# Two-layer graph network on one core: when GpSimd's inner products and VectorE's turned one-hot run in the second sweep

## The chip, the cores and the metric

One core of a Trainium2 chip. The metric is the device time of one execution in microseconds; less is better. Every engine of the core (TensorE, VectorE, ScalarE, GpSimd, SyncE) runs its own list of instructions in order, and the lists are tied together by semaphores alone. In the profile they are called PE (with PEld for its weight loads), DVE, ACT, POOL and SP.

## The reference

20,000 directed edges join 1,250 nodes with 512 features each. Layer 0 is an attention sum over edges; layer 1 is a message layer whose features are 128 scalars and 128 vectors of three components. Each is added to its input and normalized. The second sweep computes, for every edge, the part of layer 1 below:

```python
ip1 = jnp.einsum('eum,eum->eu', p1[edge_dst], p1[edge_src]) / 3.0
s0 = jnp.concatenate([pd0, pd0, ip1], axis=-1)
...
w = ssp(edge_attr @ W_f1) @ W_f2 * (ssp(s0 @ W_s1) @ W_s2)
w1, w2, w3, w4 = jnp.split(w, 4, axis=-1)
x0e, x1e = split_irreps(x[edge_src])
out0 = w1 * x0e * sh0[:, None] + w4 * (jnp.einsum('eum,em->eu', x1e, sh1) / jnp.sqrt(3.0))
out1 = w2[:, :, None] * x0e[:, :, None] * sh1[:, None, :] + w3[:, :, None] * x1e * sh0[:, None, None]
out = jax.ops.segment_sum(edge_feat, edge_dst, num_segments=old_x.shape[0])
```

`ssp` is softplus minus log 2. The names edge_dst and edge_src are the two ends of an edge: sums go to the one, features are gathered from the other. Everything is float32.

## The kernel before

The kernel first sorts the edges into groups: 88 groups of 256 slots, each group with edges of one block of 128 receiving nodes only. A slot is an edge or is empty. After the sort come the first sweep (layer 0), a stage over nodes that writes a table of 896 numbers for each node to DRAM (`tab_d`), the second sweep (layer 1), and a last stage over nodes.

The second sweep does the 88 groups one after another; a group is two tiles of 128 edges (index k). A step of a group g is a small function on one engine, and the helper `pipelined` writes the steps out in a fixed order. For its iteration i it goes through the engine's list of pairs (lag, step) and issues step(i - lag). So the order in the list is the order in the engine's queue, and lag says how many iterations a step stands behind. The loop is unrolled by U = 8.

The steps that matter here, with their lines:

- SyncE, `load`: the edges' data (`ed`), their receiving nodes turned to run along the free dimension (`ilb`), and features (`hcat`), eight groups ahead.
- GpSimd, `gather` (line 1028): two indirect DMAs fetch the table rows of the 256 source nodes into a ring of R = 4 groups (`xj`, in the tensor `ring`). `dots` (lines 1037, 1040, 1042): one product and two additions make the inner product of the vector part with the edge's three components, into `dot`, two groups deep.
- TensorE: `sources` (line 1095) spreads the receiving nodes' vectors over the edges, using the turned one-hot; `inner` (line 1054) transposes and adds VectorE's products; `hidden` (1081, 1083); `factors` (1108); `sums` (1066, 1068, 1070) adds up messages by receiving node with the one-hots as weights.
- ScalarE: `factor_out` (1151) copies a factor from PSUM, `inner_out`, `log_part` (softplus in parts), and `scaled_rows` (1121), six scaled copies of the one-hots.
- VectorE, in the order of its queue: `one_hot` (lines 1205 and 1206, two instructions for each of two tiles, SBUF to SBUF), `weights` (1174), `messages` (1181, 1184, 1189, the last of which needs `dot`), `softplus` (1169), `accumulate` (1196, adds TensorE's sums to `acc`), `turned_one_hot` (1215, `ohT` from `ilb`, SBUF to SBUF), `products` (1164, PSUM times the gathered rows, for `inner`).

The lags: in VectorE's iteration i stand one_hot, weights and messages of group i-3, softplus of i-2, accumulate of i-4, turned_one_hot of i, products of i-1. In GpSimd's iteration i stand gather of i and dots of i-2. What ties GpSimd to the others is this:

```python
if not first(g, R):
    gp.wait_ge(msg_ready, g - (R - 1))     # in gather: its ring slot is free
...
gp.wait_ge(xj_in[c], n * 32)               # in dots: the rows have landed
after(gp, msg_ready, g - 1)                # dot's buffer is free
```

`after(engine, semaphore, count)` waits until the semaphore has reached count, and does nothing for a count known to be zero or less. `oh_ready` goes up by one when a group's four one-hot instructions are done, `msg_ready` when its last message instruction is. `accumulate` waits for `sum_ready`, which TensorE raises at the end of `sums`; `products` waits for the gathered rows (`xj_in`) and for `pi_ready` of `sources`.

Of the kernel before, what the change touches and what calls it, by code (L numbers as in the profile page):

```python
# [30 lines left out]
U = 8  # L31
# [10 lines left out]
def build(nc, x, src, dst, edge_rows, W, b, a, W_pre0, b_pre0, W_pre1, W_nd0, b_nd0, W_nd1, W_g1, b_g1,  # L42
          W_g2, b_g2, W_f1, W_f2, W_s1, W_s2, W_o0, b_o0, W_o1, out):
    ctx = ExitStack()
    with ctx:
        def sb(name, shape, dt=F32, scope=ctx):
            return scope.enter_context(nc.sbuf_tensor(name, shape, dt))

        def sem(name):
            return ctx.enter_context(nc.semaphore(name))  # L50

        def after(eng, s_, count):

            if not (isinstance(count, int) and count <= 0):
                eng.wait_ge(s_, count)
# [43 lines left out]
        ring = sb("ring", [P, max(R * 2 * TW, U * 2 * XT)])  # L99
# [464 lines left out]
        def pipelined(eng, *stages, count=NG, turn=U, ring=R):  # L564


            last = max(lag for lag, _ in stages)
            peel = turn * max(-(-last // turn), 1)
            for i in range(peel):
                for lag, step in stages:  # L570
                    if i >= lag:
                        step(i - lag, (i - lag) % turn, (i - lag) // ring + 1)
            with eng.Fori(0, (count - peel) // turn) as j:  # L573
                for i in range(turn):
                    for lag, step in stages:
                        g0 = peel + i - lag
                        step(j * turn + g0, g0 % turn, j * (turn // ring) + (g0 // ring + 1))
            for i in range(count, count + last):
                for lag, step in stages:
                    if i - lag < count:  # L580
                        step(i - lag, (i - lag) % turn, (i - lag) // ring + 1)
# [5 lines left out]
        def first(g, m):  # L587
            return isinstance(g, int) and g < m
# [385 lines left out]
        oh_ready = sem("oh_ready")  # L974
# [26 lines left out]
        with nc.Block() as block:  # L1001
# [15 lines left out]
            @block.gpsimd  # L1017
            def _(gp):
                def gather(g, c, n):
                    r = c % R  # L1020

                    gp.wait_ge(ed2[c], n * 64)
                    gp.sem_inc(issue2, 1)
                    if not first(g, R):
                        gp.wait_ge(msg_ready, g - (R - 1))
                        gp.sem_inc(issue2, 1)
                    for k in range(2):
                        gp.indirect_dma_start(xj[:, r, k, :], None, tab_d[:, :],  # L1028
                                              bass.IndirectOffsetOnAxis(ap=ed[:, c, k, JD:JD + 1].bitcast(I32), axis=0))\
                          .then_inc(xj_in[c], 16)  # L1030

                def dots(g, c, n):

                    r, u = c % R, c % 2
                    gp.wait_ge(xj_in[c], n * 32)
                    after(gp, msg_ready, g - 1)
                    gp.tensor_tensor(dot[:, u, :, :, :], xj[:, r, :, P:D].rearrange("p k (m n) -> p k m n", m=3),  # L1037
                                     ed[:, c, :, IL + 2:IL + 5].unsqueeze(3).to_broadcast([P, 2, 3, P]), ALU.mult).then_inc(dot_mul, 1)
                    gp.wait_ge(dot_mul, g + 1)
                    gp.tensor_tensor(dot[:, u, :, 0, :], dot[:, u, :, 0, :], dot[:, u, :, 1, :], ALU.add).then_inc(dot_add, 1)  # L1040
                    gp.wait_ge(dot_add, g + 1)
                    gp.tensor_tensor(dot[:, u, :, 0, :], dot[:, u, :, 0, :], dot[:, u, :, 2, :], ALU.add).then_inc(dot_ready, 1)
                pipelined(gp, (0, gather), (2, dots), ring=U)

            @block.tensor
            def _(pe):
# [110 lines left out]
            @block.vector  # L1157
            def _(v):
                def products(g, c, n):
                    r = c % R  # L1160
                    v.wait_ge(xj_in[c], n * 32)
                    v.wait_ge(pi_ready, g + 1)
                    after(v, ip_ready, g)
                    v.tensor_tensor(prod[:, :, :], psB, xj[:, r, :, D:TW], ALU.mult).then_inc(prod_ready, 1)  # L1164

                def softplus(g, c, n):

                    v.wait_ge(ln_done, g + 1)
                    v.scalar_tensor_tensor(hcat[0:2 * HID, c, :], psH, 0.0, lx[:, :], ALU.max, ALU.add).then_inc(sp_done, 1)  # L1169

                def weights(g, c, n):

                    v.wait_ge(s_copied, g + 1)
                    v.tensor_tensor(psF, S_sb[:, :, :], psF, ALU.mult).then_inc(w_done, 1)  # L1174

                def messages(g, c, n):
                    r, u = c % R, c % 2

                    v.wait_ge(w_done, g + 1)
                    after(v, sum_ready, g - 1)  # L1180
                    v.tensor_tensor(mm_sb[:, u, :, 0:D + P].rearrange("p k (s n) -> p k s n", n=P)[:, :, 0:5:4, :],
                                    psF[:, :, 0:2 * P].rearrange("p k (s n) -> p k s n", n=P),
                                    xj[:, r, :, 0:P].unsqueeze(2).to_broadcast([P, 2, 2, P]), ALU.mult)
                    v.tensor_tensor(mm_sb[:, u, :, P:D].rearrange("p k (m n) -> p k m n", m=3),  # L1184
                                    psF[:, :, 2 * P:3 * P].unsqueeze(2).to_broadcast([P, 2, 3, P]),
                                    xj[:, r, :, P:D].rearrange("p k (m n) -> p k m n", m=3), ALU.mult)

                    v.wait_ge(dot_ready, g + 1)
                    v.tensor_tensor(mm_sb[:, u, :, D + P:D + 2 * P], psF[:, :, 3 * P:D], dot[:, u, :, 0, :], ALU.mult).then_inc(msg_ready, 1)  # L1189

                def accumulate(g, c, n):
                    blk_r = v.value_load(gblk[0:1, bass.ds(g, 1)], min_val=0, max_val=NB - 1)
                    v.wait_ge(sum_ready, g + 1)
                    after(v, acc2_done, g)
                    dst_ = acc[:, bass.ds(blk_r, 1), 0:D].rearrange("p b n -> p (b n)")
                    v.tensor_tensor(dst_, dst_, psA, ALU.add).then_inc(acc2_done, 1)  # L1196

                def one_hot(g, c, n):

                    u = c % 2  # L1200
                    v.wait_ge(ed2[c], n * 64)
                    after(v, oh_sh_ready, g - 1)
                    after(v, sum_ready, g - 1)
                    for k in range(2):
                        v.tensor_scalar(oh[:, u, k, :], iota[:, :], ed[:, c, k, IL:IL + 1], None, ALU.is_equal)  # L1205
                        ins = v.tensor_scalar(ohs[:, u, k, 0, :], iota[:, :], ed[:, c, k, IL:IL + 1], ed[:, c, k, IL + 1:IL + 2],  # L1206
                                              ALU.is_equal, ALU.mult)
                    ins.then_inc(oh_ready, 1)

                def turned_one_hot(g, c, n):  # L1210

                    u = c % 2
                    v.wait_ge(ed2[c], n * 64)
                    after(v, hid_ready, g - 1)
                    v.tensor_scalar(ohT[:, u, :], ilb[:, c, :], pcol[:, 0:1], None, ALU.is_equal).then_inc(ohT_ready, 1)
                pipelined(v, (3, one_hot), (3, weights), (3, messages), (2, softplus), (4, accumulate), (0, turned_one_hot),
                          (1, products), ring=U)


# [139 lines left out]
```

## Time and profile before

| | before |
|---|---|
| median of 3 runs | 1291.41 us (1288.12 to 1293.72) |
| profiled execution | 1291.39 us |
| its span in the profile | 1289.7 us |
| TensorE busy, whole span | 999.7 us, 78% |
| VectorE busy | 939.1 us, 73% |
| ScalarE busy | 546.3 us, 42% |
| GpSimd busy | 794.0 us, 62% |

The page of the profile gives busy times over the whole span. The second sweep runs from about 555 us to about 1245 us of it; a table by stretches cuts such a part out. A round is the time from one group's step to the next group's same step. A line in a timeline has the start in us, the duration in us, engine, line, operation, output and inputs, the count of merged instructions, and in brackets the idle time of the engine before it with what ended it.

### The profile page before, as it was taken

Reading aid. Unit: us, or ns where it says so; the run is one execution under the profiler, and the core shown is the slowest. Engines: PE = TensorE matmul, PEld = TensorE weight load, DVE = VectorE, ACT = ScalarE, POOL = GpSimd, SP = SyncE. Lnnn points to the kernel's source line nnn. Section 1 sums busy time; section 2 is a strip of 40 time slices with the busy share of each in tenths; the row PEclk is TensorE's granted clock in tenths of the full one; section 3 lists DMA queues with packets and bytes.
Section 4 is the critical chain, followed back from the end, with each engine's and each line's share of the span. In section 5 each row is a group of like instructions: output and inputs, shape, how many; then the busy total and the mean of one; then the engine's idle time right before and its main releaser. Section 6 shows DMA issues by size and latency. Waiting matters only on the chain. (4 is left out here: it accounts for less than half of the span.)

```text
span 1289.7 us, 23680 instructions
## 1 busy us (share of the span) xinstructions
PE 999.7 (78%) x5530; PEld 643.5 (50%) x5531; DVE 939.1 (73%) x2190; ACT 546.3 (42%) x1559; POOL 794.0 (62%) x809
## 2 busy tenths in 40 slices
PE   2227445499999967748999889999999999998874
PEld 1213222255555546625656555565565655655554
DVE  7250101378777758538999999989999899999967
ACT  2213210123233326525555555555555555555541
POOL 3777777577777711256666666666666666666622
PEclk9757678699999989859999999999999999999997
DMA  9201101588777831154544444544444444444302
GB/s 346 57 15 32 32 23 57 146 242 241 238 241 237 242 66 57 66 191 149 155 145 139 139 144 148 158 141 143 151 151 143 142 148 149 153 141 139 114 1 82
DMA packets 109167, 177.46 MB, mean 138 GB/s; under 512 B 40191, under 2 KB 79343, under 8 KB 109009
## 3 DMA queue, kind: packets, MB, share of 16 engines
q0 software_dynamic: 33184, 130.15, 31.3%
q1 hardware_dynamic: 72752, 45.60, 12.3%
q10 hardware_dynamic: 3200, 1.38, 0.5%
q8 instruction: 11, 0.18, 0.1%
q14 instruction: 20, 0.16, 0.0%
HBM read 157.31 MB, written 19.74 MB: 137 GB/s over the span
## 5 line engine op out<-in xcount | busy, mean ns | idle before, releaser
L1028 POOL DMA_INDIRECT ring<-tab_d,ed x176 | 181.4, 1030 | 232.8 <-DVE mm_sb L1189 168.7
L698 PE MATMUL ps<-ring,aw 128*128 128x512 f32 x352 | 195.7, 644 | 18.6 <-DVE aw L649 16.9
L618 POOL DMA_INDIRECT ring<-xt_d,ed x176 | 168.0, 955 | 61.4 <-issue 43.9
L1121 ACT ACTIVATE ohs<-oh,ed 128x128 f32<-128x128 f32 x528 | 171.7, 389 | 77.2 <-DVE ohs L1206 77.1
L375 POOL DMA_INDIRECT slots_d<-stage,stage_pos x157 | 153.5, 978 | 66.3 <-issue 48.7
L1066 PE MATMUL ps<-mm_sb,ohs 128*128 128x512 f32 x352 | 189.4, 620 | 1.4 <-DVE acc L1196 1.4
L1068 PEld LDWEIGHTS ps<-mm_sb,ohs 128*128 128x128 f32 x1056 | 145.6, 191 | 84.3 <-issue 84.3
L1151 ACT ACTIVATE S_sb<-ps 128x512 f32<-128x512 f32 x176 | 95.5, 595 | 132.0 <-PE ps L1108 132.0
L1068 PE MATMUL ps<-mm_sb,ohs 128*128 128x128 f32 x1056 | 146.2, 275 | 0.0
L1037 POOL TENSOR_TENSOR dot<-ring,ed 128x768 f32<-128x768 f32 x88 | 130.3, 1480 | 10.2 <-DVE mm_sb L1189 7.3
L1108 PE MATMUL ps<-w,hcat 32*128 32x512 f32 x704 | 102.0, 648 | 27.1 <-DVE hcat L1169 27.1
L1054 PEld LDWEIGHTS ps<-ident,prod 128*128 128x128 f32 x528 | 57.7, 143 | 119.8 <-DVE prod L1164 106.5
L1054 PE MATMUL ps<-ident,prod 128*128 128x128 f32 x528 | 78.7, 286 | 46.2 <-DVE prod L1164 46.1
L699 PEld LDWEIGHTS ps<-ring,aw 128*128 128x128 f32 x352 | 67.6, 192 | 85.8 <-issue 85.8
L1174 DVE TENSOR_TENSOR ps<-S_sb,ps 128x1024 f32<-128x1024 f32 x88 | 107.0, 1216 | 1.8 <-ACT S_sb L1151 1.8
L1205 DVE TENSOR_SCALAR oh<-iota,ed 128x128 f32<-128x128 f32 x176 | 105.3, 598 | 0.0
L1206 DVE TENSOR_SCALAR ohs<-iota,ed 128x128 f32<-128x128 f32 x176 | 98.1, 557 | 0.0
L661 DVE TENSOR_TENSOR acc<-acc,ps 128x513 f32 x88 | 60.7, 690 | 39.5 <-issue 24.4
L1164 DVE TENSOR_TENSOR prod<-ps,ring 128x768 f32<-128x768 f32 x88 | 83.3, 947 | 6.7 <-DMA ring<-tab_d,ed 6.7
L1196 DVE TENSOR_TENSOR acc<-acc,ps 128x512 f32 x88 | 59.8, 680 | 35.2 <-PE ps L1070 35.2
L1184 DVE TENSOR_TENSOR mm_sb<-ps,ring 128x768 f32<-128x768 f32 x88 | 83.4, 947 | 0.0
L284 DVE CAST stage<-loc_i 128x16 f32<-128x16 int32 (+1 forms) x10 | 1.8, 182 | 103.4 <-DMA slots_d<-stage,stage_pos 103.2
(194 smaller groups left out, 1878.0 us busy)
## 6 DMA issues: line engine op xcount, KB each, us to landing
ilb<-f_d SPq DMA_DIRECT2D x88, 128.0 KB, 3.7
ed<-slots_d SPq DMA_DIRECT2D x176, 38.0 KB, 3.0
tab_d<-tabrow SPq DMA_DIRECT2D x5, 896.0 KB, 3.7
slots_d<-fill SPq DMA_DIRECT2D x8, 418.0 KB, 4.4
f_d<-ft SPq DMA_DIRECT2D x88, 38.0 KB
ring<-xt_d,ed POOLq DMA_INDIRECT x176, 4.1
hcat<-f_d SPq DMA_DIRECT2D x176, 16.0 KB, 4.2
ring<-tab_d,ed POOLq DMA_INDIRECT x176, 4.9
```

What stands on the lines that cost most here:

```text
L375: g.indirect_dma_start(slots_d[:, :], bass.IndirectOffsetOnAxis(ap=stage_pos[:, h, k:k + 1], axis=0), stage[:, h, k, :], None).then_inc(sc ...
L618: gp.indirect_dma_start(xg[:, c, k, :], None, xt_d[:, :], bass.IndirectOffsetOnAxis(ap=ed[:, c, k, JD:JD + 1].bitcast(I32), axis=0))\
L698: pe.matmul(ps[:, 2 * u, :], aw[:, r, k, :], xg[:, c, k, 0:D], start=(k == 0), stop=(k == 1))
L1028: gp.indirect_dma_start(xj[:, r, k, :], None, tab_d[:, :], bass.IndirectOffsetOnAxis(ap=ed[:, c, k, JD:JD + 1].bitcast(I32), axis=0))\
L1037: gp.tensor_tensor(dot[:, u, :, :, :], xj[:, r, :, P:D].rearrange("p k (m n) -> p k m n", m=3), ed[:, c, :, IL + 2:IL + 5].unsqueeze(3).to ...
L1054: mm = pe.matmul(psI[:, P * k:P * k + P], prod[:, k, P * m:P * m + P], ident[:, :], is_transpose=True, start=(m == 0), stop=(m == 2))
L1066: pe.matmul(psA, ohs[:, u, k, 0, :], mm_sb[:, u, k, 0:D], start=(k == 0), stop=False)
L1068: pe.matmul(psA[:, P * (m + 1):P * (m + 2)], ohs[:, u, k, m + 1, :], mm_sb[:, u, k, D:D + P], start=False, stop=False)
L1108: mm = pe.matmul((psS if q < 2 else psF)[:, q % 2, :], hcat[rows, c, :], w2[rows, :], start=True, stop=True)
L1121: ins = act.activation(ohs[:, u, k, m, :], oh[:, u, k, :], ACT.Copy, scale=ed[:, c, k, IL + 1 + m:IL + 2 + m])
L1174: v.tensor_tensor(psF, S_sb[:, :, :], psF, ALU.mult).then_inc(w_done, 1)
L1205: v.tensor_scalar(oh[:, u, k, :], iota[:, :], ed[:, c, k, IL:IL + 1], None, ALU.is_equal)
```

## The change

Two edits, both in the second sweep. GpSimd's `dots` of group g waits, besides the rest, for `oh_ready` to reach g (the one-hots of group g-1), and `dots` comes ahead of `gather` in GpSimd's list. In VectorE's list `turned_one_hot` comes ahead of `accumulate`. No instruction that computes or moves data is added or removed.

```diff
                     gp.wait_ge(xj_in[c], n * 32)
+                    after(gp, oh_ready, g)
                     after(gp, msg_ready, g - 1)
...
-                pipelined(gp, (0, gather), (2, dots), ring=U)
+                pipelined(gp, (2, dots), (0, gather), ring=U)
...
-                pipelined(v, (3, one_hot), (3, weights), (3, messages), (2, softplus), (4, accumulate), (0, turned_one_hot),
+                pipelined(v, (3, one_hot), (3, weights), (3, messages), (2, softplus), (0, turned_one_hot), (4, accumulate),
                           (1, products), ring=U)
```

GpSimd's queue in the unrolled loop of the second sweep, before (each L1028 pair is a gather, L1037 to L1042 one `dots`; the semaphores in brackets are those waited for):

```order
L1028 DMA ring<-tab_d,ed 128x896 [waits ed2_3,msg_ready]
L1028 DMA ring<-tab_d,ed 128x896
L1037 TENSOR_TENSOR dot<-ring,ed 128x768 [waits msg_ready,xj_in1]
L1039 REGISTER_ALU
L1040 TENSOR_TENSOR dot<-dot 128x2x128 [waits dot_mul]
L1042 TENSOR_TENSOR dot<-dot 128x2x128 [waits dot_add]
```

The same place in the changed kernel (whose lines from 1036 on stand one higher):

```order
L1038 TENSOR_TENSOR dot<-ring,ed 128x768 [waits msg_ready,oh_ready,xj_in3]
L1040 REGISTER_ALU
L1041 TENSOR_TENSOR dot<-dot 128x2x128 [waits dot_mul]
L1043 TENSOR_TENSOR dot<-dot 128x2x128 [waits dot_add]
L1028 DMA ring<-tab_d,ed 128x896 [waits ed2_5,msg_ready]
L1028 DMA ring<-tab_d,ed 128x896
```

The gather of an iteration stood ahead of its `dots` and stands behind it now, and `dots` waits for `oh_ready`.

VectorE's queue in the second sweep, from the softplus to the first one-hot of the next iteration, before:

```order
L1169 SCALAR_TENSOR_TENSOR hcat<-ps,lx 64x128 [waits ln_done]
L1192 TENSOR_LOAD gblk
L1192 ISA x2
L1196 ISA [waits acc2_done,sum_ready]
L1196 TENSOR_TENSOR acc<-acc,ps 128x512
L1215 TENSOR_SCALAR ohT<-ilb,pcol 128x256 [waits hid_ready,ed2_5]
L1164 TENSOR_TENSOR prod<-ps,ring 128x768 [waits ip_ready,pi_ready,xj_in4]
```

And in the changed kernel:

```order
L1170 SCALAR_TENSOR_TENSOR hcat<-ps,lx 64x128 [waits ln_done]
L1216 TENSOR_SCALAR ohT<-ilb,pcol 128x256 [waits hid_ready,ed2_5]
L1193 TENSOR_LOAD gblk
L1193 ISA x2
L1197 ISA [waits acc2_done,sum_ready]
L1197 TENSOR_TENSOR acc<-acc,ps 128x512
L1165 TENSOR_TENSOR prod<-ps,ring 128x768 [waits ip_ready,pi_ready,xj_in4]
```

The turned one-hot has moved from between the accumulation and the products to the place ahead of the accumulation's wait for `sum_ready`.

## Rows read from the trace of the kernel before

**Rows 1.** Busy by stretch: length, PE, PEld, DVE, ACT, POOL, PEclk, DMA, GB/s

```profile
610.00:1240.00 630.00, 569.98 (x3778) 374.41 (x3775) 581.05 (x987) 359.53 (x1067) 407.59 (x405) 1.00 0.45 141
```

**Rows 2.** Line 1164, 610 to 1233 us: min/median/max ns, first, last start

```profile
L1164 DVE TENSOR_TENSOR prod<-ps,ring x82: 942/948/957, 610.2 to 1231.9; 128x768 f32<-128x768 f32 x82
```

**Rows 3.** Waits from 610 to 1233 us: us in total, times, longest

```profile
POOL ring L1028 <- DVE mm_sb L1189: 154.3, 39, 4.0
...
PE ps L1054 <- DVE prod L1164: 34.7, 81, 1.3
```

**Rows 4.** Timeline of VectorE, two rounds of the second sweep

```profile
910.26 0.94 DVE L1164 TENSOR_TENSOR prod<-ps,ring 128x768 f32<-128x768 f32 x1
911.12 0.27 DVE L1205 TENSOR_SCALAR oh<-iota,ed 128x128 f32<-128x128 f32 x1
...
911.77 0.33 DVE L1206 TENSOR_SCALAR ohs<-iota,ed 128x128 f32<-128x128 f32 x1
...
915.57 0.28 DVE L1169 SCALAR_TENSOR_TENSOR hcat<-ps,lx 64x128 f32<-64x128 f32 x1 [0.40 <-ACT lx L1139]
916.54 0.69 DVE L1196 TENSOR_TENSOR acc<-acc,ps 128x512 f32 x1 [0.69 <-PE ps L1070]
917.15 0.35 DVE L1215 TENSOR_SCALAR ohT<-ilb,pcol 128x256 fp32r<-128x256 f32 x1
917.41 0.95 DVE L1164 TENSOR_TENSOR prod<-ps,ring 128x768 f32<-128x768 f32 x1
918.28 1.64 DVE L1205 TENSOR_SCALAR oh<-iota,ed 128x128 f32<-128x128 f32 x1
...
921.49 1.22 DVE L1174 TENSOR_TENSOR ps<-S_sb,ps 128x1024 f32<-128x1024 f32 x1
...
925.60 0.94 DVE L1164 TENSOR_TENSOR prod<-ps,ring 128x768 f32<-128x768 f32 x1
```

**Rows 5.** Timeline of GpSimd beside the same two rounds

```profile
911.50 0.99 POOL L1028 DMA_INDIRECT ring<-tab_d,ed  x1 [0.30 <-issue]
912.51 1.48 POOL L1037 TENSOR_TENSOR dot<-ring,ed 128x768 f32<-128x768 f32 x1
...
914.87 0.72 POOL L1042 TENSOR_TENSOR dot<-dot 128x256 f32<-128x256 f32 x1
916.09 0.98 POOL L1028 DMA_INDIRECT ring<-tab_d,ed  x1 [0.49 <-issue]
...
918.35 1.48 POOL L1037 TENSOR_TENSOR dot<-ring,ed 128x768 f32<-128x768 f32 x1
```

**Rows 6.** Line 1174 from 640 to 1200 us, as in rows 2

```profile
L1174 DVE TENSOR_TENSOR ps<-S_sb,ps x73: 1210/1215/1229, 644.9 to 1195.3; 128x1024 f32<-128x1024 f32 x73
```

**Rows 7.** Timeline of TensorE, a round in the middle and one of the last

```profile
911.25 0.87 PE L1054 MATMUL ps<-ident,prod 128*128 128x128 f32 x6 [0.54 <-DVE prod L1164]
...
1225.97 0.87 PE L1054 MATMUL ps<-ident,prod 128*128 128x128 f32 x6 [1.26 <-DVE prod L1164]
...
1231.72 1.14 PE L1108 MATMUL ps<-w,hcat 32*128 32x512 f32 x8
1232.90 0.88 PE L1054 MATMUL ps<-ident,prod 128*128 128x128 f32 x6
```

**Rows 8.** Timeline of VectorE in that last round, without a turned one-hot

```profile
1231.25 0.69 DVE L1196 TENSOR_TENSOR acc<-acc,ps 128x512 f32 x1 [0.69 <-PE ps L1070]
1231.89 0.96 DVE L1164 TENSOR_TENSOR prod<-ps,ring 128x768 f32<-128x768 f32 x1
```

**Rows 9.** Line 1028, 640 to 1200 us, and its transfers to landing

```profile
L1028 POOL DMA_INDIRECT ring<-tab_d,ed x147: 948/997/1434, 639.4 to 1199.3; - x147
...
DMA to landing us min/median/max: 3.7/4.9/5.9
```

**Rows 10.** Timeline of VectorE at the start of the second sweep

```profile
569.14 1.75 DVE L1215 TENSOR_SCALAR ohT<-ilb,pcol 128x256 fp32r<-128x256 f32 x1
...
585.07 2.31 DVE L1215 TENSOR_SCALAR ohT<-ilb,pcol 128x256 fp32r<-128x256 f32 x1
```

## The prediction

> **What bounds the kernel now.** The table by stretches comes first: the second sweep's long stretch [rows 1] takes 630 of 1289.7 us, TensorE at full clock, with VectorE busy 92% and TensorE 90% of it, so neither engine alone is the limit. The rows on line 1164 [rows 2] give the length of a round: 82 products from 610.2 to 1231.9, so 81 rounds in 621.7 us, 7.68 us each. The table of waits [rows 3] shows TensorE waiting for those products in nearly every round, and GpSimd waiting 39 times, up to 4.0 us, for the messages: it works in bursts, every second round.
>
> VectorE's timeline [rows 4] shows why. Two kinds of round alternate. From the products at 910.26 to those at 917.41 are 7.15 us, and the four one-hot instructions run from 911.12 to 912.10, 0.98 us. The next round, to 925.60, takes 8.19 us: the first one-hot alone takes 1.64 us instead of 0.27, and the block runs from 918.28 until the weights start at 921.49, 3.2 us. GpSimd's timeline [rows 5] has the partner: its inner products start at 918.35 in the slow block, but at 912.51 in the quick one, just after the one-hots. So a one-hot (both operands in SBUF, no second tensor) stands still while GpSimd runs a tensor_tensor; the weights don't, their spread is 1210 to 1229 ns in 73 rounds [rows 6], though the inner products lie beside them in every second one. The slow round loses 2.3 us on VectorE, and half of that appears in the loop (8.19 - 7.15 = 1.04), since TensorE has work to go on with.
>
> TensorE sets the rest. The last rounds, in which there is no gather and no turned one-hot left, show its pace [rows 7, 8]: transposes of the products at 1225.97, factors at 1231.72, next transposes at 1232.90, that is 6.93 us. In it the accumulation starts 5.28 us after the transposes, as the sums end, the products 0.64 us later, and the next transposes 1.01 us after the products' start.
>
> **The change part by part.**
>
> 1. GpSimd's inner products wait for the one-hots of VectorE's round. The count fits: inner products g need one_hot(g-1), which VectorE does in its iteration g+2, the same in which GpSimd reaches inner products g. They are not due until messages(g), a round later, so the wait closes no circle. They take 3.08 us (912.51 to 914.87 + 0.72) [rows 5]. VectorE's next operation in the fast form, the turned one-hot, comes after the softplus, which ended at 915.85, 3.75 us after the last one-hot [rows 4]. So 3.08 us fit, with 0.67 us for signals. Every round becomes the quick kind: 8.19 to 7.15 in each second one, 0.52 us a round on average. Queued behind the wait are GpSimd's own additions and gathers; who waits for them is item 2.
>
> 2. The gather comes behind the inner products. GpSimd's work per round is 3.08 us, a gap of 0.5 (915.59 to 916.09), and two gathers of about 1.0 with 0.3 between [rows 5], 5.9 us: less than 6.93, so GpSimd is not the bound. The second gather is issued about 4.9 us after the one-hots end (3.08 + 0.5 + 1.3), and the products that need it come in the next round: 12.0 us after the same point (one-hots end 0.85 us after the transposes' start at 911.25 [rows 7]; products at 6.93 + 5.92). 7.1 us are left for a landing of 4.9 median, 5.9 at most [rows 9]. Before, it was issued a round or so earlier. I cost it at nothing; its cover is those 2.2 us.
>
> 3. The turned one-hot goes ahead of the accumulation. Today VectorE idles 0.69 us for the sums [rows 4] and then runs the accumulation (0.61), the turned one-hot (0.26) and the products in line: 0.87 us from the accumulation's start to the products'. In the last rounds, without a turned one-hot between, it is 0.64 [rows 8]. The 0.35 us instruction fits in the 0.69 us of idle time. This takes 0.23 us off the chain sums, accumulation, products, transposes: 7.15 to about 6.93, the pace seen in [rows 7]. Zero is the lower bound of this term, if TensorE's sources (ready just before 1231.89) already hold the products; 0.26, the whole instruction, the upper. I take 0.23, because the row at 1231.89 is this very order.
>
> 4. The start of the sweep. Two turned one-hots were held there by the inner products: 1.75 and 2.31 us instead of 0.35 [rows 10]. The new wait keeps the inner products away: 1.4 + 2.0 = 3.4 us. Four rounds before 610.2 gain too, but the gather of round 2 now goes out behind the first inner products, some 6 us later, and may make its products wait about 1 us. I take 4 us, with 2 and 7 as ends.
>
> **The sum.** 81 x (7.68 - 6.93) = 60.5, by the unrounded 7.676. With 4 at the start: 64.5 us. The profiled execution took 1291.39 us (span 1289.7), the median of the runs is 1291.41, so the two may be taken as one: 1291.4 - 64.5 = 1227. Other stages are not touched. The least round that I would grant is 6.85 (TensorE's factors end at 1232.86, the transposes begin at 1232.90 [rows 7], so TensorE has hardly any idle time left): 67 + 7, 1217 us. With rounds of 7.05 and 2 at the start: 1239 us. That is the forecast's own range.
>
> **A rule that speaks against it.** The trace has one-hots inside a gather: the gather at 911.50 took 0.99 us, the one-hots at 911.77 and at 911.12 were at their shortest [rows 4, 5], and line 1028's spread is 948 to 1434 ns [rows 9]. So the one-hots don't wait for a gather, and a gather waits at most 0.4 us. In the new order the turned one-hot starts 4.5 us after the transposes, and the gathers begin then as well. By this row that costs nothing. The Trainium skill, page "SBUF — State Buffer", section "Who interferes with whom", says that a VectorE instruction in a two-port mode and a GpSimd instruction exclude each other for a whole instruction, whichever came first. Taken to the letter it would have the turned one-hot stand behind a gather, the second rival below; the row above speaks against that.
>
> **The rivals.**
>
> A. Only the wait pays, since the products are held by something else than the turned one-hot (the sources). Every round stays at the 7.15 or 7.16 of today's quick kind: 81 x 0.52 = 42, with 3 at the start, 1246 us. For it: the products' input from TensorE ends only shortly before they start. Against it: 0.64 us at 1231.25 [rows 8]. Chance 0.14.
>
> B. The gather holds the turned one-hot. It would run from 5.43 (gather from 4.45, 0.98 long) to 5.70, the accumulation starts at 5.70 instead of 5.28, the products at 6.30, the transposes at 7.31: 81 x 0.37 + 4 = 34 us, 1258 us. Chance 0.06.
>
> C. It ends slower: the gather lands late. With a landing L, two rounds are then tied to one-hots, 4.9 + L, products to the end of the next one-hots 1.85: 2 x round = 6.75 + L. It decides above L = 7.1 us, and beats today's 7.68 only below L = 8.6. At L = 9 the round is 7.87 and the time 1291 + 81 x 0.2 = 1307 us. Against it: 5.9 at most in 147 gathers, at a DMA load of 45% [rows 1, 9]. Chance 0.04.
>
> D. The change doesn't do what it says: the inner products still meet the one-hots, because GpSimd falls behind and starts late. It would have to lose 1 us a round over its 5.9. Rounds then remain near 7.5 to 7.68: 1275 to 1292 us. Chance 0.08, about half of it inside 0.5% of no change.
>
> **How the numbers follow.** My forecast has 0.68. 0.5% is 6.5 us, about what a measurement of this kernel can tell from no change. Faster by more: the forecast, A, B and half of D, 0.92. Within it: 0.04. Slower: C, 0.04. The range of 8 in 10 takes in the forecast's own range and A: 1216 to 1250 us. B, C and D are left out, 0.18.
>
> **What would show it.** The one-hots' two lines (1205 and 1206 today) should fall from means near 0.6 us to 0.27 and 0.33; rounds should all be alike, 6.9 to 7.0 us; GpSimd should wait for the one-hots each round, about 1 us; accumulation to products 0.6 us; TensorE busy over 98% of the sweep; VectorE's share about 85%. It is wrong on item 1 if one-hots above 0.5 us remain, on item 3 if the rounds stand at 7.15, on item 2 if the products wait for the ring's DMA.

## The result, and the profile after

The changed kernel takes 1228.39 us in the median (1226.63 to 1229.83, 4 runs) beside 1291.16 us before (1288.12 to 1293.72, 4 runs): ratio 0.9508, 95% interval 0.9486 to 0.9531. That is 62.8 us less; 1227 was forecast, with 1216 to 1250 as range. The profiled execution took 1229.83 us, its span is 1228.1 us.

From the page of the changed kernel, the busy times over the span, and five groups of instructions (lines from 1036 on stand one higher than before):

```profile
PE 995.1 (81%) x5530; PEld 642.5 (52%) x5531; DVE 854.4 (70%) x2190; ACT 533.3 (43%) x1559; POOL 780.0 (64%) x809
...
L1038 POOL TENSOR_TENSOR dot<-ring,ed 128x768 f32<-128x768 f32 x88 | 129.6, 1473 | 134.1 <-issue 109.8
...
L1028 POOL DMA_INDIRECT ring<-tab_d,ed x176 | 170.4, 968 | 62.2 <-issue 30.5
...
L1175 DVE TENSOR_TENSOR ps<-S_sb,ps 128x1024 f32<-128x1024 f32 x88 | 108.2, 1229 | 28.0 <-ACT S_sb L1152 26.8
...
L1197 DVE TENSOR_TENSOR acc<-acc,ps 128x512 f32 x88 | 60.6, 688 | 45.7 <-PE ps L1071 45.7
...
L1165 DVE TENSOR_TENSOR prod<-ps,ring 128x768 f32<-128x768 f32 x88 | 83.6, 950 | 6.8 <-DMA ring<-tab_d,ed 6.8
```

VectorE is busy for 85 us less, with the same 2190 instructions, and GpSimd now idles ahead of its inner products (L1038), 134.1 us, and less ahead of the gather, 62.2 us where it was 232.8. VectorE now idles ahead of the weights (L1175), and ahead of the accumulation (L1197) in every round instead of every second. The products wait for a DMA once, at the start, as before.

The lines of the one-hots over the whole span, then of the products from 605 to 1200 us (count, shortest, median and longest in ns, first and last start), the last answering to [rows 2]:

```profile
L1206 DVE TENSOR_SCALAR oh<-iota,ed x176: 267/278/330, 570.0 to 1175.3; 128x128 f32<-128x128 f32 x176
...
L1207 DVE TENSOR_SCALAR ohs<-iota,ed x176: 329/340/361, 570.2 to 1175.5; 128x128 f32<-128x128 f32 x176
...
L1216 DVE TENSOR_SCALAR ohT<-ilb,pcol x88: 333/336/354, 554.4 to 1159.6; 128x256 fp32r<-128x256 f32 x88
...
L1165 DVE TENSOR_TENSOR prod<-ps,ring x81: 948/950/956, 610.9 to 1167.9; 128x768 f32<-128x768 f32 x81
```

No one-hot is held any longer: the longest of 176 takes 0.36 us, where 1.98 us was the longest before. 80 rounds take 557.0 us, 6.96 us each, beside 7.68.

A round of the changed kernel, VectorE's timeline first, then GpSimd's, to be read against [rows 4, 5]:

```profile
904.91 0.34 DVE L1207 TENSOR_SCALAR ohs<-iota,ed 128x128 f32<-128x128 f32 x1
905.57 1.23 DVE L1175 TENSOR_TENSOR ps<-S_sb,ps 128x1024 f32<-128x1024 f32 x1 [0.32 <-ACT S_sb L1152]
...
908.72 0.28 DVE L1170 SCALAR_TENSOR_TENSOR hcat<-ps,lx 64x128 f32<-64x128 f32 x1
908.92 0.34 DVE L1216 TENSOR_SCALAR ohT<-ilb,pcol 128x256 fp32r<-128x256 f32 x1
909.71 0.69 DVE L1197 TENSOR_TENSOR acc<-acc,ps 128x512 f32 x1 [0.46 <-PE ps L1071]
910.32 0.95 DVE L1165 TENSOR_TENSOR prod<-ps,ring 128x768 f32<-128x768 f32 x1
911.18 0.28 DVE L1206 TENSOR_SCALAR oh<-iota,ed 128x128 f32<-128x128 f32 x1
```

```profile
905.39 1.47 POOL L1038 TENSOR_TENSOR dot<-ring,ed 128x768 f32<-128x768 f32 x1 [1.44 <-issue]
906.94 0.73 POOL L1041 TENSOR_TENSOR dot<-dot 128x256 f32<-128x256 f32 x1
907.75 0.73 POOL L1043 TENSOR_TENSOR dot<-dot 128x256 f32<-128x256 f32 x1
908.62 0.98 POOL L1028 DMA_INDIRECT ring<-tab_d,ed  x1
909.91 0.95 POOL L1028 DMA_INDIRECT ring<-tab_d,ed  x1 [0.30 <-issue]
```

The inner products start 0.14 us after the last one-hot's end (905.25) and are done at 908.48, before the turned one-hot at 908.92. The profile files most of GpSimd's idle time here under issue and names the one-hots for 20.8 us of it alone; that it waits for them is read from the 0.14 us and from the queue. The turned one-hot fits in ahead of the sums, with 0.46 us of idle time left, and 0.61 us after the accumulation's start the products begin.

TensorE's timeline in the same stretch:

```profile
904.40 0.87 PE L1055 MATMUL ps<-ident,prod 128*128 128x128 f32 x6
...
910.17 1.14 PE L1109 MATMUL ps<-w,hcat 32*128 32x512 f32 x8
911.33 0.87 PE L1055 MATMUL ps<-ident,prod 128*128 128x128 f32 x6
```

6.93 us from transposes to transposes, as in the last round of before [rows 7]. From 610 to 1170 us TensorE is busy 554.85 of 560 us and VectorE 491.36.

### The profile page after: what moved, and what is told of

Same layout as the page of the kernel before. It is cut to its first block and busy times, and to the rows that moved or that the text cites. A ratio compares the mean times of both kernels' runs of the same rounds, so it can differ in the third digit from the quotient of the medians.

```text
span 1228.1 us, 23671 instructions
## 1 busy us (share of the span) xinstructions
PE 995.1 (81%) x5530; PEld 642.5 (52%) x5531; DVE 854.4 (70%) x2190; ACT 533.3 (43%) x1559; POOL 780.0 (64%) x809
## 5 line engine op out<-in xcount | busy, mean ns | idle before, releaser
L1038 POOL TENSOR_TENSOR dot<-ring,ed 128x768 f32<-128x768 f32 x88 | 129.6, 1473 | 134.1 <-issue 109.8
L1028 POOL DMA_INDIRECT ring<-tab_d,ed x176 | 170.4, 968 | 62.2 <-issue 30.5
L1175 DVE TENSOR_TENSOR ps<-S_sb,ps 128x1024 f32<-128x1024 f32 x88 | 108.2, 1229 | 28.0 <-ACT S_sb L1152 26.8
L1197 DVE TENSOR_TENSOR acc<-acc,ps 128x512 f32 x88 | 60.6, 688 | 45.7 <-PE ps L1071 45.7
L1096 PE MATMUL ps<-p1h,ohT 128*128 x176 | 67.7, 385 | 10.3 <-DVE ohT L1216 10.0
L630 DVE SCALAR_TENSOR_TENSOR junk<-iota,ed,srow 128x128 f32<-128x128 f32 x176 | 54.9, 348 | 24.7 <-DMA ed<-slots_d 18.5
```

The lines of the kernel that those rows point to most:

```text
L1028: gp.indirect_dma_start(xj[:, r, k, :], None, tab_d[:, :], bass.IndirectOffsetOnAxis(ap=ed[:, c, k, JD:JD + 1].bitcast(I32), axis=0))\
```

## The experiments

Twelve kernels were run, each timed beside the kernel before on the same chip. The time in the table is the median; the round is worked out from the products' line of each trace (last start less first start, by the rounds between).

| run | edit | us | ratio to before, 95% interval | round, us |
|---|---|---|---|---|
| changed kernel | | 1228.4 | 0.9508, 0.9486 to 0.9531 | 6.96 |
| e1_no_swap | without VectorE's swap | 1249.4 | 0.9663, 0.9635 to 0.9691 | 7.20 |
| e2_swap_only | VectorE's swap alone | 1295.4 | 1.0022, 1.0009 to 1.0036 | 7.72 |
| e3_gather_first | the wait, but gather first | 1229.7 | 0.9508, 0.9481 to 0.9535 | 6.97 |
| e4_no_wait | both orders, no wait | 1259.7 | 0.9750, 0.9721 to 0.9778 | 7.28 |
| e5_collide | inner products on the one-hots | 1283.9 | 0.9941, 0.9925 to 0.9958 | 7.58 |
| e6_odd_form | the same, one-hots in an odd shape | 1233.7 | 0.9547, 0.9512 to 0.9581 | 6.99 |
| e7_light_sources | 0.34 us less for TensorE | 1231.5 | 0.9542, 0.9507 to 0.9578 | 6.97 |
| e8_sources_early | sources and products earlier | 1220.3 | 0.9446, 0.9415 to 0.9478 | 6.84 |
| e9_pe_order_only | sources earlier alone | 1285.8 | 0.9946, 0.9926 to 0.9966 | 7.62 |
| e10_dve_order_only | products earlier alone | 1235.7 | 0.9560, 0.9534 to 0.9586 | 7.03 |
| e11_early_and_light | e8 and e7 together | 1191.1 | 0.9218, 0.9198 to 0.9239 | 6.48 |
| e12_before_odd_form | kernel before, odd shape alone | 1248.6 | 0.9661, 0.9640 to 0.9682 | 7.20 |

### The change taken apart: e1 to e4

**e1_no_swap** is the changed kernel with VectorE's old order:

```diff
-(2, softplus), (0, turned_one_hot), (4, accumulate),
+(2, softplus), (4, accumulate), (0, turned_one_hot),
```

> The changed kernel with VectorE's old order (accumulation, then turned one-hot); GpSimd's two edits stay. Theory (the wait saves 0.52 us a round, the swap 0.23): every round is the quick kind of before, 7.15 us, against 6.96 in the changed kernel: 1228.4 + 81 x 0.2 = 1245 us. Rival (the swap is idle, the products are held by TensorE's sources): 1228 us. One-hots at 0.27 and 0.33 us in both.

Measured: 1249.4 us, 21 us above the changed kernel, and a round of 7.20. Its one-hots' medians are 279 and 342 ns, 288 and 349 at most. So the wait by itself removes the collisions with the inner products, and the swap is worth 0.24 us a round on top of it: the rival, that the products are held by the sources, falls. Up to 2 of the 21 us have another cause. From 605 to 1190 us 80 turned one-hots run beside a gather's instruction, and nine of them took 0.55 or 0.56 us. They are those that start 0.50 or 0.51 us after its start, and they end 0.1 us after its end:

```profile
901.50 0.95 POOL L1028 DMA_INDIRECT ring<-tab_d,ed  x1 [0.30 <-issue]
902.01 0.55 DVE L1216 TENSOR_SCALAR ohT<-ilb,pcol 128x256 fp32r<-128x256 f32 x1
```

The other 71 start 0.37 to 0.40 us after it and take 0.35 us at most.

**e2_swap_only** is the kernel before with the same pair exchanged the other way.

> The kernel before with only VectorE's swap. Theory: in the slow rounds VectorE is busy without a gap from the one-hots to the products, so the order there changes nothing; in every second, quick round the swap saves 0.25 us: 41 x 0.25 = 10, 1281 us, one-hots still at means near 0.6 us. Rival (the two edits add up freely, 0.23 us in each of 81 rounds): 1272 us. Rival (swap idle): 1291 us.

Measured: 1295.4 us, 0.2% slower than before (1292.5 us beside it). The theory and the first rival missed; the second, that the swap is idle, had nearly the time, but the rounds are not those of before. VectorE's timeline shows what none of them had, first the end of the one-hots' block and then GpSimd's rows of the same time:

```profile
903.76 0.27 DVE L1205 TENSOR_SCALAR oh<-iota,ed 128x128 f32<-128x128 f32 x1
903.95 0.33 DVE L1206 TENSOR_SCALAR ohs<-iota,ed 128x128 f32<-128x128 f32 x1
904.21 0.27 DVE L1205 TENSOR_SCALAR oh<-iota,ed 128x128 f32<-128x128 f32 x1
904.40 2.15 DVE L1206 TENSOR_SCALAR ohs<-iota,ed 128x128 f32<-128x128 f32 x1
906.49 1.21 DVE L1174 TENSOR_TENSOR ps<-S_sb,ps 128x1024 f32<-128x1024 f32 x1
...
912.10 2.16 DVE L1206 TENSOR_SCALAR ohs<-iota,ed 128x128 f32<-128x128 f32 x1
```

```profile
904.02 0.95 POOL L1028 DMA_INDIRECT ring<-tab_d,ed  x1 [0.30 <-issue]
904.98 1.49 POOL L1037 TENSOR_TENSOR dot<-ring,ed 128x768 f32<-128x768 f32 x1
906.55 0.73 POOL L1040 TENSOR_TENSOR dot<-dot 128x256 f32<-128x256 f32 x1
```

The alternation is gone: every round is alike and has its collision, in the last of the four one-hots (904.40, 912.10, 919.80). That one-hot, in line from 904.40, is done at 906.55, past the whole first instruction of the inner products (904.98 to 906.47), though it had its turn before it. GpSimd's start follows from the end of the messages, 902 or so, plus two gathers. My reading, which no run tests by itself, is that a slightly shorter round moves that start from one spot of VectorE's queue to another, and that the held one-hot in turn sets the next start. An edit elsewhere could then lose or gain by shifting the meeting point, which the changed kernel's explicit wait rules out.

**e3_gather_first** keeps the wait and undoes GpSimd's order:

```diff
-pipelined(gp, (2, dots), (0, gather), ring=U)
+pipelined(gp, (0, gather), (2, dots), ring=U)
```

> The changed kernel with GpSimd's gather ahead of the inner products again; the wait for the one-hots stays. Theory: the wait alone does it. The gather's slot comes free with the messages, about 4.4 us into the round, which is when the inner products end, so it goes out at the same time in either order: 1228 us within 3. Rival (the reordering is needed, since a gather that is issued first delays the inner products beyond the room for them): 1240 us or more, with turned one-hots of over 0.5 us.

Measured: 1229.7 us, the same ratio to before as the changed kernel, 0.9508. With the wait in place the reordering of GpSimd's list is worth nothing. One cost of it is seen: from 605 to 1175 us 58 one-hots (L1207) start 0.54 to 0.60 us after the start of a gather's instruction; they take 0.39 to 0.45 us instead of 0.34 and end 0.03 to 0.06 us after it has ended.

**e4_no_wait** keeps both orders and drops the one line `after(gp, oh_ready, g)`.

> The changed kernel without the wait for the one-hots; inner products ahead of the gather and VectorE's swap stay. Theory: the inner products then start with the end of the messages, 4.5 us into the round, and run for 3.1 us, across the turned one-hot (held for about 1.5 us) and the first one-hot (held about 0.8): a round of about 7.9 us, no quick rounds left: 1228.4 + 81 x 0.95 = 1305 us, slower than before. Rival (the reordering by itself spaces GpSimd's work well enough): 1230 to 1250 us.

Measured: 1259.7 us, between the two. The inner products do start with the messages' end, and the turned one-hot is held in every round:

```profile
L1215 DVE TENSOR_SCALAR ohT<-ilb,pcol x81: 935/1197/1635, 608.7 to 1191.5; 128x256 fp32r<-128x256 f32 x81
```

Its median is 1.20 us instead of 0.34. But the first one-hot was not held (the median of L1205 is 273 ns from 605 to 1200 us, 332 at the most), since the delay pushes the one-hots behind the end of the inner products. The expectation had charged both; the order alone loses 31 us against the changed kernel, not 77. Taken together: with the wait, GpSimd's order is worth nothing (e3) and the swap 21 us (e1). Without the wait the same order is worth 36 us (e2 beside e4, 1295.4 and 1259.7), as it moves the inner products from the one-hots to the turned one-hot. So half of the gain can be had without the wait, and the parts do not add up.

### What is held, and by what: e5, e6, e12

**e5_collide** lets the inner products start with the one-hots on purpose:

```diff
-after(gp, oh_ready, g)
+gp.wait_ge(prod_ready, g + 1)
```

> The changed kernel, but the inner products of group g wait for the products of group g instead of the one-hots of group g-1: they then start together with the one-hots in every round, not in every second. Theory (a tensor_tensor of GpSimd makes the one-hots stand still): block of one-hots 3.2 us instead of 0.98 in each round, round about 8.2 us: 1228.4 + 81 x 1.25 = 1330 us. Rival (the gain came from even spacing of GpSimd's bursts and not from the collision): about 1230 us, since GpSimd's work is as evenly spaced here.

Measured: 1283.9 us, 55 us more than the changed kernel with the same instructions, the same spacing on GpSimd and the same orders. VectorE's timeline:

```profile
903.44 0.27 DVE L1206 TENSOR_SCALAR oh<-iota,ed 128x128 f32<-128x128 f32 x1
903.63 1.56 DVE L1207 TENSOR_SCALAR ohs<-iota,ed 128x128 f32<-128x128 f32 x1
905.12 0.27 DVE L1206 TENSOR_SCALAR oh<-iota,ed 128x128 f32<-128x128 f32 x1
905.32 0.81 DVE L1207 TENSOR_SCALAR ohs<-iota,ed 128x128 f32<-128x128 f32 x1
906.05 1.21 DVE L1175 TENSOR_TENSOR ps<-S_sb,ps 128x1024 f32<-128x1024 f32 x1
```

The block takes 2.6 us and not the 3.2 expected: the first one-hot slips through ahead of GpSimd's start (903.60), and GpSimd's third instruction, at 906.12, finds the block over. Direction and place were right. The block's excess over 0.98 us was put a third too large (2.2 for 1.6), and the time at nearly twice its size (101 us more expected, 55 measured): VectorE's idle time ahead of the weights and the accumulation, 0.78 us a round in the changed kernel, takes up a part, and such idle time is gone here. The spacing rival falls.

**e6_odd_form** leaves the inner products on the one-hots and changes only the one-hots' shape:

```diff
+v.tensor_copy(iota3[:, 0:2, 0:43], iota[:, 0:86].rearrange("p (a b) -> p a b", a=2))
...
-v.tensor_scalar(oh[:, u, k, :], iota[:, :], ...
+v.tensor_scalar(oh[:, u, k, :].rearrange("p (a b) -> p a b", a=3), iota3[:, :, 0:43], ...
```

> As e5_collide, but the one-hots read their row of numbers as 3 x 43 elements with a gap, and write 129 contiguous ones (one unused column), still SBUF to SBUF. Theory (only the fast form, about two elements a cycle, is held, and this shape keeps VectorE off it): each one-hot takes 0.07 us longer, none is held, and the time is 1228 to 1245 us though the inner products lie on top of them. Rival (any VectorE instruction with both operands in SBUF is held, or the shape is still run in the fast form): as e5_collide, 1330 us.

Measured: 1233.7 us. The two lines, from the table of groups (busy us, mean ns, idle before), and GpSimd's inner products right upon them:

```profile
L1215 DVE TENSOR_SCALAR ohs<-iota,ed 128x129 f32<-128x129 f32 x166 | 66.3, 400 | 0.0
...
L1214 DVE TENSOR_SCALAR oh<-iota,ed 128x129 f32<-128x129 f32 x166 | 56.2, 338 | 0.0
```

```profile
901.24 0.40 DVE L1215 TENSOR_SCALAR ohs<-iota,ed 128x129 f32<-128x129 f32 x1
901.55 0.34 DVE L1214 TENSOR_SCALAR oh<-iota,ed 128x129 f32<-128x129 f32 x1
901.80 0.40 DVE L1215 TENSOR_SCALAR ohs<-iota,ed 128x129 f32<-128x129 f32 x1
```

```profile
901.15 1.47 POOL L1040 TENSOR_TENSOR dot<-ring,ed 128x768 f32<-128x768 f32 x1 [1.27 <-DVE prod L1167]
```

Each one-hot pays 0.06 us for one column more and the slower form, and none is held (means of 338 and 400 ns over 166). Operands in SBUF on both sides are thus not enough for the collision; the fast form is needed. The Trainium skill, page "VectorE: DVE Perf Modes", section "What auto-detection actually checks", says that the two-port mode for float32 wants a single source and a destination in SBUF whose outermost dimensions are both even or equal. By it 3 against 129 is neither, if the unbroken destination counts as one row of 129 (no row of the profile shows that); the times, 338 ns instead of 0.27 us, agree.

**e12_before_odd_form** puts that shape, and nothing else, into the kernel before.

> The kernel before with nothing changed but the shape of the one-hots, as in e6_odd_form (3 x 43 with a gap into 129 contiguous elements), both orders and no wait on one-hots as before. Theory (the fast form is what collides): no one-hot is held, every round is the quick kind of before, 7.15 to 7.2 us: 1291.5 - 81 x 0.5 = 1250 us. Rival (the slow rounds have another cause): 1291 us plus 0.07 us for each of four one-hots in 81 rounds, 1300 us or more.

Measured: 1248.6 us, 43 us below before, and the round, 7.20, is that of e1_no_swap. Two different cures of the collision, a wait and a shape, end at the same 1249 us: that is the collision's price in the kernel before, 43 us. With the swap and a collision in every round it is 50 us (e5 beside e6).

### What bounds the round now: e7 to e11

**e7_light_sources** leaves out the second pass of TensorE's sources (the low part of the node vectors, a loss of precision in ip1):

```diff
-for part, tab in enumerate((p1h, p1l)):
+for part, tab in enumerate((p1h,)):
```

> The changed kernel with the second of the two passes of TensorE's sources left out (the low part of the node vectors, so ip1 has lower precision): 0.34 us less for TensorE in each round, behind the sums and ahead of the factors. Theory (the chain transposes, sums, accumulation, products, transposes sets the round): that chain does not go through the sources, the round stays at 6.9 and the time at 1225 to 1228 us. Rival (TensorE's own work is the bound): 81 x 0.34 = 27 us less, 1201 us.

Measured: 1231.5 us, round 6.97, no gain. TensorE now idles in each round, for the products:

```profile
906.68 0.87 PE L1055 MATMUL ps<-ident,prod 128*128 128x128 f32 x6 [0.36 <-DVE prod L1165]
```

So TensorE, busy 99% in the changed kernel, was not its bound: 0.34 us of work taken away turned into 0.36 us of idle time.

**e8_sources_early** takes the accumulation out of the chain:

```diff
-pipelined(pe, (2, inner), (4, sums(0)), (2, hidden), (4, sums(1)), (1, sources), (2, factors), ring=U)
+pipelined(pe, (2, inner), (4, sums(0)), (2, hidden), (1, sources), (4, sums(1)), (2, factors), ring=U)
...
-(0, turned_one_hot), (4, accumulate), (1, products)
+(0, turned_one_hot), (1, products), (4, accumulate)
```

> The changed kernel with two further moves: TensorE's sources ahead of the second half of the sums, VectorE's products ahead of the accumulation. The accumulation is then out of the chain and only TensorE's own work is left. Theory: the round falls from 6.96 to what TensorE needs back to back, 6.82 to 6.89: 1217 to 1223 us. Rival (TensorE is back to back already): 1228 us. Rival (the accumulation comes too late and holds the next round's sums or one-hots): 1235 us or more.

Measured: 1220.3 us, round 6.84: a version that beats both kernels, with nothing left out. TensorE's work runs without a break, and the products start at 905.21, two microseconds ahead of their reader:

```profile
905.21 0.94 DVE L1165 TENSOR_TENSOR prod<-ps,ring 128x768 f32<-128x768 f32 x1
906.42 0.69 DVE L1197 TENSOR_TENSOR acc<-acc,ps 128x512 f32 x1 [0.27 <-PE ps L1071]
```

```profile
900.43 0.87 PE L1055 MATMUL ps<-ident,prod 128*128 128x128 f32 x6
...
906.20 1.14 PE L1109 MATMUL ps<-w,hcat 32*128 32x512 f32 x8
907.27 0.87 PE L1055 MATMUL ps<-ident,prod 128*128 128x128 f32 x6
```

**e9_pe_order_only** and **e10_dve_order_only** are its two halves.

> The changed kernel with TensorE's sources ahead of the second half of the sums, VectorE's order as in the changed kernel. Theory (the chain sums, accumulation, products, transposes sets the round): the sums end 0.85 us later in the round, so the chain grows by that much: 6.93 + 0.85 = 7.78 us, 1228.4 + 81 x 0.85 = 1297 us. Rival (TensorE's amount of work alone counts, its order does not): 1228 us or, as in e8_sources_early, 1220 us.

Measured: 1285.8 us, round 7.62. The accumulation starts later in the round, 5.98 us after the transposes' start (898.12) instead of 5.31, and everything behind it too:

```profile
904.10 0.69 DVE L1197 TENSOR_TENSOR acc<-acc,ps 128x512 f32 x1 [1.12 <-PE ps L1071]
904.71 0.95 DVE L1165 TENSOR_TENSOR prod<-ps,ring 128x768 f32<-128x768 f32 x1
```

The mechanism holds; the shift was 0.66 us a round (7.62 beside 6.96), not the 0.85 taken.

> The changed kernel with VectorE's products ahead of the accumulation, TensorE's order as in the changed kernel. Theory: the products now wait for the sources, which end 5.9 us into the round, so they start where they start now, and the accumulation behind them has 0.7 us of room: 1228 us within 4. Rival (the products start earlier and e8_sources_early owes its gain to this move alone): 1220 us. Rival (the late accumulation pushes the one-hots back): 1240 us.

Measured: 1235.7 us, round 7.03, a little slower than the changed kernel, and outside the 1228 within 4 that was expected. That the products wait for the sources, 0.97 us in this row, is as the theory has it; where the 0.07 us a round go is not shown:

```profile
900.79 0.96 DVE L1165 TENSOR_TENSOR prod<-ps,ring 128x768 f32<-128x768 f32 x1 [0.97 <-PE ps L1096]
901.71 0.69 DVE L1197 TENSOR_TENSOR acc<-acc,ps 128x512 f32 x1
```

Alone, one half loses 57 us and the other 7; together they win 8.

**e11_early_and_light** joins e8 with e7's lighter sources (the same part of ip1 left out).

> e8_sources_early with the second pass of the sources left out (lower precision of ip1), 0.35 us less work for TensorE in each round. Theory (in e8_sources_early TensorE's own work is the bound): 1220.3 - 81 x 0.35 = 1192 us. Rival (another chain of about the same length stands behind it, such as factors, ScalarE's copy, weights, messages, softplus, some 6.2 us): above 1200 us.

Measured: 1191.1 us, round 6.48. The same 0.34 us that were worth nothing in e7 are worth 29 us here (0.36 us a round), so in e8 TensorE is the bound. The chain through the accumulation was the bound of the changed kernel, a tenth of a microsecond a round above it (6.96 beside 6.84).

## Why the prediction was right, point by point

- **Item 1, the wait.** The collision was named with its place, its partner and its form; e1 and e12 price it at 43 us, where rival A, which was this part alone, had 45. Room for the inner products: 3.09 us (905.39 to 908.48) and 0.14 us for the signal, against 3.67 us from the last one-hot's end to the turned one-hot.
- **Item 2, the gather behind.** Costed at nothing, and beside the wait e3 shows nothing. The second gather goes out 4.7 us after the one-hots (905.25 to 909.91; 4.9 was taken) and landings from 600 to 1150 us were 3.6, 4.3 and 6.1 us (least, median, most) beside [rows 9]; no products waited for it but the very first. What the working overstated is the gap between inner products and gather, 0.14 us instead of 0.5, so GpSimd idles for 1.44 us a round and not for one.
- **Item 3, the swap.** 0.23 us was taken from one row of the last rounds [rows 8]; e1 measures 0.24. Not seen was that the swap alone is worth nothing or less (e2), and that GpSimd's order, costed at nothing, is worth 36 us where the wait is missing (e4). The sum did not need this, but the prediction treated the items as independent, and they are not.
- **Item 4, the start.** Group 6's products come at 603.58 instead of 610.17: 6.6 us, with 4 taken and 7 as upper end. The cost charged for the second round's late gather did not appear.
- **The sum.** From group 6 to the last group 81 rounds took 564.4 us (603.58 to 1167.94) instead of 621.7 [rows 2]: 57.4 us less, where 60.5 was taken (81 x 0.746 is 60.4). Seven rounds in eight take 6.92 us and the eighth, where the unrolled loop turns, 7.27 (610.86 to 617.79, and 659.32 to 666.59), which the row of the last rounds could not show. With the start, 64.0 us were gained by the end of the sweep against 64.5 in the sum. That they meet so closely is luck: 3.1 us too much in the rounds and 2.6 too little at the start cancel. The span shows 61.6: from the last products to the end it is 60.2 us now and was 57.8, all of it in the last stage over nodes, whose code the change doesn't touch. The trace shows where 1.8 us of these 2.4 lie: a VectorE instruction of the one-hots' kind (tensor_scalar, SBUF to SBUF), 0.55 us long before, comes just behind a GpSimd tensor_tensor and is held.

```profile
1199.49 2.11 POOL L1304 TENSOR_TENSOR ya<-acc,xt 128x1024 f32 x1 [1.69 <-PE ps L1314]
1199.66 2.35 DVE L1255 TENSOR_SCALAR hb<-x 128x768 f32 x1
```

  In the kernel before VectorE's came first (1263.02 beside 1263.46) and was not held. It is the same collision in another stage, which neither the prediction nor the change looked at; the profiles of e3, e6, e8 and e11 have it too. Another 0.8 us are a longer wait of VectorE for TensorE in that stage (6.21 us instead of 5.40). TensorE's granted clock there was 0.72 of full speed in this execution and 0.75 in that of before; whether that is the cause is not tried.
- **The rule against it.** In the changed kernel a gather did not hold the turned one-hot: that one ran at 908.92 for 0.34 us inside the gather of 908.62 to 909.60, and 354 ns is the longest of 88. But the prediction read too much from its row, a one-hot 0.27 us behind a gather's start, when it said that one-hots don't wait for a gather. The changed kernel's turned one-hots stand 0.22 to 0.40 us behind such a start. In e1 those at 0.50 us were held for 0.2 us, in e3 one-hots at 0.54 to 0.60 us for 0.1. So rival B's mechanism exists, with a hold of 0.2 us where B took one of 0.9. That the change stays clear of it by 0.1 us was not worked out: in this part the prediction had luck. For GpSimd's tensor instructions the Trainium skill's lock for the whole instruction (page "SBUF — State Buffer", section "Who interferes with whom") is what e5 and e6 show, but for which of the two goes first: there the recorded starts of e2 do not fit it. For its DMA instructions the rows show a hold of 0.2 us at most, for a gather of 0.95. As the changed kernel's bound B falls, C falls with the landings, D with the one-hots' lines, A with e1.
- **What would show it.** Of the list, rounds that are "all alike" was wrong by the eighth one, and VectorE's share is 88% (491.36 of 560), not 85. TensorE's 99% was forecast and could have misled: e7 shows that it was not the bound.

## What to carry to other kernels

When an instruction of a fixed shape has two durations, look for what the other engines run at that moment before counting its work; a semaphore that puts the partner beside instructions that don't mind is free where the partner has slack. Price the edits of a change together, since one that shortens a chain pays only after the collision on it is gone, and may otherwise just move the meeting point. Look for the same pair of instructions in every stage: the last one lost 1.8 us to it here, unnoticed. An engine busy 99% isn't the bound until taking work away from it moves the time.

## What the runs showed of the hardware that was not expected

- A gather holds a fast-form VectorE instruction too, but only one that starts in a certain part of it: 0.37 to 0.40 us behind its start, 0.35 us (71 of e1); 0.50 or 0.51 us behind it, 0.55 or 0.56 us (9 of e1); 0.80 to 0.86 us behind it, 0.28 or 0.29 us, as if undisturbed (59 of e3).
- A fast-form VectorE instruction can be held by a GpSimd tensor instruction that starts after its own recorded start: 904.40 against 904.98 in e2, done at 906.55. The record's start may lie ahead of the real one; what was argued from "who came first" doesn't fit these rows, and this stays open.
- The loser is not always VectorE. In e5 GpSimd's second instruction took 0.85 us instead of 0.73 beside a one-hot.
- A shape that is 0.06 us slower an instruction made the kernel before 43 us faster (e12).
- The turn of the unrolled loop costs 0.35 us every eighth round of the changed kernel. In the kernel before, the same round is one of the slow ones and no longer than they are (8.20 us, 671.55 to 679.75).
